# An attention and mixture-of-experts block: attention and dense part in one program block, shared expert two batches later, a ring of three PSUM banks

## The reference

```python
h = layernorm(x) * (1 + ca) + sa
# attention layer on h
n = layernorm(h) * g1 + b1
Q, K, V = n @ qU @ qV + qb, n @ kU @ kV + kb, n @ vU @ vV + vb   # 16 heads x 8
attn = softmax(where(causal, Q K^T / sqrt(8), -1e9))
h1 = h + (attn @ V) @ out_U @ out_V + out_b
h2 = h1 + gelu(layernorm(h1) @ fc1 + fc1_b) @ fc2 + fc2_b
x = x + ga * h2
# experts on h3
h3 = layernorm(x) * (1 + cb) + sb
n3 = h3 * rsqrt(mean(h3**2) + 1e-8) * norm_weight
shared = relu(n3 @ sw1 + sb1) @ sw2 + sb2
probs = sigmoid(n3 @ router_w.T); best two, weights normalised
routed = sum of two of: relu(n3 @ ew1[e] + eb1[e]) @ ew2[e] + eb2[e]
out = x + gb * (shared + routed)
```

## Time and profile before

| | |
|---|---|
| median of 3 runs (lowest, highest) | 858.69 us (856.99, 859.17) |
| the profiled execution | 858.44 us, of which the span 856.7 |
| clock granted to PE, mean | 0.932 |
| PE busy / weight loads | 672.8 us / 408.3 us |
| DVE, ACT, POOL busy | 450.7, 427.7, 306.0 us |

### The profile page before, as it was taken

One profiled execution on the slowest core, in us unless ns is written; L12 is line 12 of the kernel. 1 busy time (PEld: TensorE's weight loads), 2 busy tenths in 40 slices (PEclk: granted clock), 3 DMA queues, 4 the chain that ended last, 5 costly groups with the idle time before them and its releaser, 6 DMA issues. The chain is left out here.

```text
span 856.7 us, 15853 instructions
## 1 busy us (share of the span) xinstructions
PE 672.8 (79%) x5361; PEld 408.3 (48%) x5361; DVE 450.7 (53%) x1304; ACT 427.7 (50%) x749; POOL 306.0 (36%) x492
## 2 busy tenths in 40 slices
PE   4457899989898998989844588898665899999920
PEld 3223343333433343444312456666545788888820
DVE  1558787868587666767413345777541222222217
ACT  5120567665665666656731367677223445445500
POOL 2332323142433323313123227656730444444420
PEclk9999899999999999999975889999887999999975
DMA  8334232333332334311133601111124767767719
GB/s 157 108 106 153 83 105 89 119 114 115 119 108 100 116 100 141 111 66 56 52 105 121 161 28 54 44 51 42 58 79 137 202 194 207 200 199 202 204 36 280
DMA packets 98448, 101.07 MB, mean 118 GB/s; under 512 B 13152, under 2 KB 81672, under 8 KB 98288
## 3 DMA queue, kind: packets, MB, share of 16 engines
q1 hardware_dynamic: 89360, 87.45, 34.0%
q0 software_dynamic: 4544, 9.45, 3.1%
q10 hardware_dynamic: 4480, 3.35, 1.7%
HBM read 60.54 MB, written 37.57 MB: 115 GB/s over the span
## 5 line engine op out<-in xcount | busy, mean ns | idle before, releaser
L1043 DVE TENSOR_REDUCE row_max<-ps_s 128x1 f32<-128x384 f32 (+3 forms) x384 | 216.9, 595 | 94.4 <-PE ps_s L780 74.1
L626 ACT ACTIVATE work<-ps_s 128x1024 f32<-128x1024 f32 (+1 forms) x192 | 168.4, 884 | 66.7 <-PE ps_s L809 64.0
L780 PE MATMUL ps_s<-k_st,q_st 128*128 128x384 bf16 (+3 forms) x512 | 130.7, 312 | 0.0
L1569 POOL DMA_INDIRECT y_d<-res,target x78 | 74.8, 959 | 115.5 <-DVE res L1639 103.7
L777 PE MATMUL ps_s<-later_q,ident_b 128*128 128x128 bf16 (+1 forms) x384 | 94.8, 251 | 18.0 <-DVE row_max L1043 13.5
L826 PE MATMUL ps_pv<-work,v_sb 128*32 128x512 f32 (+3 forms) x1024 | 95.2, 445 | 1.3 <-ACT ctx_raw L660 1.2
L777 PEld LDWEIGHTS ps_s<-later_q,ident_b 128*128 128x128 bf16 x384 | 37.4, 98 | 116.6 <-DVE row_max L1043 81.7
L1635 DVE TENSOR_TENSOR biased<-ps_s,bias 128x256 f32<-128x256 f32 x39 | 16.6, 425 | 130.2 <-PE ps_s L1621 127.1
L1621 PEld LDWEIGHTS ps_s<-w_tile,x_hidden 128*128 128x128 f32 x624 | 75.6, 192 | 2.0
L1611 PE MATMUL ps_s<-tok_t,w_tile 128*128 128x256 f32 x312 | 76.1, 388 | 0.0
L1621 PE MATMUL ps_s<-w_tile,x_hidden 128*128 128x128 f32 x624 | 75.8, 275 | 0.0
(11 more groups left out here) (206 smaller groups left out, 1038.4 us busy)
## 6 DMA issues: line engine op xcount, KB each, us to landing
w_tile<-in_ew SPq DMA_DIRECT2D x39, 514.0 KB
ctx_d<-ctx_raw SPq DMA_DIRECT2D x32, 256.0 KB, 2.7
q_st<-q_d SPq DMA_DIRECT2D x64, 102.0 KB
k_st<-k_d SPq DMA_DIRECT2D x64, 96.0 KB
rows<-slots_d SPq DMA_DIRECT2D x39, 132.0 KB
got<-y_d SPq DMA_DIRECT2D x16, 256.0 KB, 5.3
q_d<-qk_part SPq DMA_DIRECT2D x8, 384.0 KB, 2.5
k_d<-qk_part SPq DMA_DIRECT2D x8, 384.0 KB, 2.7
```

The source lines that it names most:

```text
L626: act.activation(dst, src, ACT.Exp, scale=SCALE).then_inc(exp_done, 1)
L780: mm = pe.matmul(bnk[:, k * keys:(k + 1) * keys], q_st[b % 2][:, g, j, i * P:(i + 1) * P], k_st[b % 2][:, g, j // 2, 0:keys], start=False, ...
L1043: dve.reduce_max(row_max[:, m % 2, js[0] % 2, j:j + len(js), i], src, AXIS.X).then_inc(max_taken, 1)
L1569: pool.indirect_dma_start(y_d[:], bass.IndirectOffsetOnAxis(ap=target[:, k, c:c + 1], axis=0), res[:, k, c, :], None).then_inc(put[k], 16)
```

## The change

**Ring of three banks.** `ps_s1` and `ps_m` become one tensor `ps_r` of three banks. Units of `s1` and all users of the single bank take their banks in turn, in the order of PE's program (`ring_order`), and each waits for the copy out of the one user before it in its bank (the last four users all take bank 2). PE's order in a step becomes: `s2`(0), `s2`(1), context 0, `s1`(0, 1), [O], `s1`(2, 3), M, `s2`(2), `s2`(3), context 1 to 3, `s1`(4, 5), [T, K, V], `s1`(6, 7), [Q], `s2`(4), `s2`(5), `s1`(8 to 11), [U]. ACT's fourth exponential and its copy of the context go ahead of the copies of T, K, V and Q. DVE's layer norm pieces stand in two lumps, behind units 3 and 7.

**One block.** `dense` is gone as a function; its code stands in `attend`'s block. Its large tiles are cut from memory of attention's that is dead by then (`arena`, `arena_early`). SP loads `x2_t` of batches 0 to 3 and all weights and gate rows in step 27 (`EARLY_STEP`), `x2_t` of 4 to 7 later, as buffers come free. Steps from 33 (`MERGE`) on are called between dense iterations: on PE 33 and 34 in n=0, 35 and 36 in n=1, 37 to 39 in n=4; on ACT 33 to 35 in n=0, 36 to 39 in n=4; on POOL 33 and 34 ahead of the first root, 35 behind it, 36, 37, 38 and 39 at the ends of n=1, 2, 3; on DVE 33 and 34 first, 35 and 36 in n=1, 37 in n=2, the rest in n=3. DVE's memset of the filler and POOL's tables wait for the last context product and stand ahead of step 33.

**Shared expert later.** `l1` and its relu are done for batch n-5 (was n-3), `l2` for n-6 (was n-4), the sum on DVE for n-7 (was n-5).

**Gate rows twice.** `gate_b` is loaded a second time, into a new tile, behind the expert loop's loads; `combine` waits for that.

```diff
@@ constants @@
 LAG = 3
 FIRST_STEP, LAST_STEP = -9, NG + 7
+MERGE, EARLY_STEP = NG + 1, NG - 5
+L1_LAG, L2_LAG = 5, 6
...
+        units(m, 0, 1)
+        one(n, "O")
+        units(m, 2, 3)
+        if 0 <= m - 1 < NG:
+            order.append(("M", m - 1))
+        units(m, 4, 5)
+        one(n, "T", "K", "V")
+        units(m, 6, 7)
+        one(n, "Q")
+        units(m, 8, 9, 10, 11)
...
+RING = ring_order()
+PLACE = {one: k for k, one in enumerate(RING)}
+RING_BANK = [k % 3 if k < len(RING) - 4 else 2 for k in range(len(RING))]
...
-    for n in range(B + 3):
-        for name, b in (("F", n), ("L", n - 3)):
+    for n in range(B + L1_LAG):
+        for name, b in (("F", n), ("L", n - L1_LAG)):
...
-        ps_s1 = pb("ps_s1", [P, 2, 512])
+        ps_r = pb("ps_r", [P, 3, 512])
         ps_pv = pb("ps_pv", [P, 512])
-        ps_m = pb("ps_m", [P, 512])
+
+        ps_m, ps_s1 = ps_r[:, 2, :], ps_r[:, 0:2, :]
...
+                        if n == EARLY_STEP:
+                            sp.wait_ge(h_ready, NT * B)
+                            sp.wait_ge(filled["V"], B)
+                            sp.wait_ge(qk_low, 2 * B)
+                            sp.wait_ge(qk_stored, 16 * 6 * B)
+                            sp.wait_ge(mod_stored, 32)
+                            sp.wait_ge(after_stored, 16 * DEEP)
+                            sp.dma_start(x2_t[:], after_d[0:DEEP].rearrange("b p s -> p b s")).then_inc(x2_loaded[0], 16)
...
+                            sp.dma_start(router_t[:], a["router_t"]).then_inc(dense_loaded, 16)
+                            sp.dma_start(shared_w1[:], a["sw1"]).then_inc(dense_loaded, 16)
...
+                    for n in range(MERGE, MERGE + 3):
+                        step(n)
+                    load_rows(4)
+                    load_rows(5)
...
@@ PE @@
                     def bank(name, k):
 
-                        wait(pe, bank_emptied, BANK[name, k])
+                        at = PLACE[name, k]
+                        same = [k for k in range(at) if RING_BANK[k] == RING_BANK[at]]
+                        if same:
+                            before = RING[same[-1]]
+                            if before[0] == "S":
+                                pe.wait_ge(max_taken, before[1] + 1)
+                            elif before in BY_ACT:
+                                pe.wait_ge(act_emptied, BY_ACT[before] + 1)
+                            else:
+                                pe.wait_ge(dve_emptied, BY_DVE[before] + 1)
+                        return ring(name, k)
...
                         s2(n, 0)
+                        s2(n, 1)
                         context(n - 1, 0)
                         s1(m, 0, 1)
-                        s2(n, 1)
-                        context(n - 1, 1)
...
                         s2(n, 2)
-                        context(n - 1, 2)
+                        s2(n, 3)
+                        for kt in range(1, NT):
+                            context(n - 1, kt)
+                        s1(m, 4, 5)
...
                         s2(n, 4)
-                        s1(m, 8, 9)
                         s2(n, 5)
-                        s1(m, 10, 11)
+                        s1(m, 8, 9, 10, 11)
...
+                    def fc2(b):
+                        pe.wait_ge(layer_emptied, LAYERS["F", b, NF - 1] + 1)
+                        wait(pe, summed, b)
+                        pe.wait_ge(ctx_out, NG)
...
+                    tail = {0: range(MERGE, MERGE + 2), 1: range(MERGE + 2, MERGE + 4), 4: range(MERGE + 4, LAST_STEP + 1)}
+                    for n in range(0, B + L2_LAG):
+                        if real(n):
+                            fc1(n)
+                        if real(n - 2):
+                            router(n - 2)
+                        if real(n - L2_LAG):
+                            l2(n - L2_LAG, 0)
+                        if real(n):
+                            fc2(n)
+                        if real(n - L2_LAG):
+                            l2(n - L2_LAG, 1)
+                        if real(n - 2):
+                            counts(n - 2)
+                        if real(n - L1_LAG):
+                            l1(n - L1_LAG)
+                        if n - 2 == B - 1:
+                            all_counts()
+                        if n in tail:
+                            for late_step in tail[n]:
+                                step(late_step)
+                        if real(n - 1):
+                            transpose_n3(n - 1)
...
@@ POOL @@
+                    tail = {1: [MERGE + 3], 2: [MERGE + 4], 3: range(MERGE + 5, LAST_STEP + 1)}
+                    for n in range(0, B + 2):
+                        if real(n - 3):
+                            scatter(n - 3)
+                        if real(n - 1):
+                            rms_of(n - 1)
+                        if n == 0:
+                            step(MERGE)
+                            step(MERGE + 1)
...
@@ DVE @@
-                        i, second = divmod(u, 2)
+                        second = u == 7
...
+                            if u in (3, 7):
                             layer_norm(n, u)
...
+                    dve.wait_ge(pv_done, NG)
                         dve.memset(fill[:, :, 0:D], 0.0).then_inc(filled_in, 1)
...
@@ experts, combine @@
+                        sp.dma_start(gate_b[:], mod_d[:, 5 * D:6 * D].partition_broadcast(P)).then_inc(gate_loaded, 16)
...
+                            if b == 0:
+                                dve.wait_ge(gate_loaded, 16)
```

More of the change, by code:

```diff
@@ L24 @@
+import math
 import struct
@@ new lines, in attend @@
+            sb2_all, router_t = early.take(D), early.take(E)
+            DENSE = 8
+            gate_rows = early.take(B, 3 * D)
+            x2_t = early.take(DEEP, S)
+            hidden = late.take(NF, S)
+            s_hidden = late.take(NF, S)
+            gated = late.take(NT, D)
+            part = late.take(NT, D)
+            x_hat = late.take(NT, D)
+            h3 = late.take(2, NT, D)
+            d_stats = sb("mlp_stats", [P, 2, NT, 6], until=front)
+            d_moments = sb("mlp_moments", [P, 2, NT, 2], until=front)
@@ new lines, in attend @@
+            neg_mean = sb("neg_mean", [P, 2, NT], until=front)
+            shift = sb("mlp_shift", [P, 2, NT], until=front)
+            d_var_eps = sb("mlp_var_eps", [P, 2, NT], until=front)
+            d_rstd = sb("mlp_rstd", [P, 2, 2, NT], until=front)
+            square = sb("square", [P, D], until=front)
+            sum_sq = sb("sum_sq", [P, 2, NT], until=front)
+            mean_sq = sb("mean_sq", [P, NT], until=front)
+            fill = late.take(FILL_ROWS // P, ROW)
+            shape = [P, NT, E]
@@ L664, in empty_after, with step @@
                         wait(act, after_stored, 16 * b)
-                        act.activation(after_t[:], ps_m[:], ACT.Identity, bias=col("ln2_b"), scale=col("ln2_g")).then_inc(bank_emptied, 1)
-                    for n in range(FIRST_STEP, LAST_STEP + 1):
+                        act.activation(after_t[:], ring("U", b), ACT.Identity, bias=col("ln2_b"), scale=col("ln2_g")).then_inc(act_emptied, 1)
+                    def step(n):
                         has = 0 <= n < NG
@@ L701, in _, with x_hat_of @@
                             qk_middle(b, 1)
+                    for n in range(FIRST_STEP, MERGE):
+                        step(n)
+                    def x_hat_of(b):
+                        act.wait_ge(x_shift, b + 1)
+                        wait(act, h3_steps, 2 * b)
+                        for i in range(NT):
+                            act.activation(x_hat[:, i, :], x_sb[:, NT * b + i, :], ACT.Identity, bias=shift[:, b % 2, i:i + 1],
+                                           scale=d_rstd[:, 0, b % 2, i:i + 1]).then_inc(x_hat_ready, 1)
```

999 lines of the change are left out of this document (496 added, 503 removed).

## The result

The changed kernel takes **823.81 us** (median of 4 runs, 822.18 to 829.58), the kernel before 858.90 beside it (4 runs): a ratio of 0.9608, 95% interval 0.9558 to 0.9658. Forecast were 845.5 us, in a range of 820 to 857, and a gain of 13; the gain is 35. The profiled execution has a span of 823.1 us, 33.6 under that of before.

What follows compares the result with a forecast made beforehand. PE was taken as nearest to full in attention, POOL's scatter chain as holding early dense batches. Sum: 858.44-27.8-4.7+3.1+0.1+16.4=845.5 us, attention at 0; range 820 to 857.

Steps and rivals of the forecast that it cites:

- Bound and seam: PE nearest to full in attention; between attention and dense part, first fc1 starts 27.8 us earlier, at 437.3.
- F(2): Start of fc1 of batch 2 in the dense part: forecast at 460, 32.5 us earlier.
- rival D: Seam does not close: last batch's chain comes late, PE waits 8 us at output product or transpose; 853, chance 0.13.
- Attention's norms among the batches: Attention's last norms, on POOL ahead of the first scatter and on DVE behind batch 0's slots, add 3.1 us.
- F(4): Start of fc1 of batch 4 in the dense part: forecast at 497, 29.4 us earlier.
- The 3.9 us more: Three POOL operations of 1.3 us meeting DVE's gates, excluding one another: 849.4 instead of 845.5; left in the range.
- Lag: Later shared expert leaves two batches behind the last count, 8.2 us each, hidden by nothing: +16.4 us.
- Rival C: Later shared expert pays: POOL's chain shrinks, batches 3 to 5 run at 12 to 13 us; 830, chance 0.09.
- F(7): Start of fc1 of batch 7: forecast at 549.7, 29.3 us earlier; from there to the last count nothing changes.
- Ring and order: Three banks and the new step order in attention: term 0, between -60 and +25 us.
- a loop of 9.3 us: Attention step's loop through DVE's reductions, POOL's split and PE's transpose of maxima; quickest windows before were 10.5 a step.
- Rival B: The ring pays: PE's waits for DVE in attention fall by a third, 20 us; 825, chance 0.24.

Runs made afterwards that it cites:

- the three with split scatters: Changed kernel, POOL's scatters two behind the mean square's root, six behind the next: 0.9558; also with the shared expert's earlier lag: 0.9395, and norm spread too: 0.9433.

## Why the prediction was wrong

- **Bound and seam: right.** Last context product to F(2) came out at 23.1 us against 55.5, the forecast -32.5 to the tenth; in the first pair it is -32.1. No wait at the output product of batch 7: rival D did not happen.
- **Attention's norms among the batches: right in place, over-sized.** The root stands ahead of the scatters, but F(2) to F(4) grew by 1.3 us where 3.1 was said. The 3.9 us more, by the exclusion that the Trainium skill, SBUF — State Buffer (section Who interferes with whom), states for such pairs, did not come either. Only one such pair met among POOL's operations of 1.3 us in the changed kernel's trace: DVE's product of two tiles in SBUF at 433.87 took 1.28 us while POOL ran its bias from 433.33 for 1.27, and the same operation at 549.70 took 0.68. The trace agrees, with 0.6 us in all.
- **Lag: right.** +15.4 measured, +16.4 forecast. Rival C, that it pays, is refuted by the kernel with the old lag. F(7) to the last count was set at 0 and is +3.5 in one pair, +1.8 in the other.
- **Ring and order: the step that failed.** The term was set at 0 between -60 and +25 and measured -19: -2.9 before the first unit (within what that start wanders by), -4.1 in the first step, which the sum did not have, -12.1 in 31 steps. For those the prediction worked out a loop of 9.3 us, added the output product, the lumps and a transpose, and held the sum of four steps, 41.6, to be the present 41.9 and 42.4. Four such steps, cut from maximum to maximum, took 42.1 and 43.0 before and take 39.5 and 40.3 now. The step with the output product takes 11.4 us where the sum has 12.0, and the three others together 28.1 and 28.9 where three loops are 27.9: the 1.7 us for lumps and transpose show only in part. And what the third bank would save was put at nothing against that sum, where PE's waits for the row maxima fell from 60 to 33 us. Only a little is given back at the transposed maxima: PE's weight loads wait there for POOL's parts 6.9 us in 16 steps, 0.6 us once before.
- **Rival B** (a third of PE's waits gone, 20 us, 825) is what happened, at a chance of 0.24, and its sign, windows of 38 to 40 us, nearly so (39.5 and 40.3). Its price has some luck in it: PE's waits fell by 27 us and the steps by 12, another 4 came in the first step, and 5 to 7 us of the gain needed the new order as well. What spoke against it, a loop of 9.3 equal to the present light step, was not a limit: the steps of before took 10.9 us on average from first to last M, the changed ones 10.5, and the shortest of those behind the first take 8.8.

## What to carry to other kernels

A loop worked out says nothing of how far above it the step runs now; cut the present steps at the same marks and measure that distance before setting a term to zero. When the fullest engine is shown busy nine tenths of the time and still waits hundreds of times for banks, neither number is the price: here the busy time fell by 16 us where the steps got longer, and 35 us fewer waits were worth 9. A bank more and an order that groups work belong together: here each order gave the shorter steps with its own number of banks. Work that is moved behind the end of a pipeline costs its full length there, here 15 us, whatever it frees in front. And where a stage gives back what an earlier one won, read the rows where it does: here it was not the queue behind, but engines that stood before finished work.

## What was unexpected of the hardware

The kernel before took medians between 847 and 860 us, 1.5% apart, with every ratio of the changed kernel between 0.956 and 0.962. The sets of runs, each on one chip, fall into two groups, and a row tells them apart. Where the kernel before takes 859 to 860 us, each of the eight traces, of before and of changed kernels, has DVE idle late in the dense part while the counts that it wants from PE are long done: 3.8 to 3.9 us before the slots of the last batch but one in five of them, 13.0 us before those of the last batch in the three with split scatters. Where it takes 847 to 849 us, none of the twelve traces has it. And when PE's next product was made ready 5 us sooner behind the last count, DVE and ACT picked up finished products late there too (578.85 to 583.25 for DVE). The cause is in none of the traces, and these rows are not all of the 12 us between the groups.
